# First set's row scores moved between the halves of the last projections

## The reference, cut to what matters

```python
x = L0_attn_a_query                                   # (2, 1024, 512) f32
x = x + _L0_attn_a_ref(_layernorm(x), Wq, Wk, Wv, Wout, lambdas, rms_weight)
x = x + _L0_ffn_ref(_layernorm(x), router_w, down_w, up_w)
x = x + _L0_attn_b_ref(_layernorm(x), ...)
x = x + _L0_ffn_ref(_layernorm(x), router_w, down_w, up_w)

# in _L0_attn_a_ref: H = 16 pairs of heads of D = 16
q = rotary((query @ Wq)); k = rotary((query @ Wk)); v = query @ Wv
attn1 = softmax(mask(q1 @ k1^T * D**-0.5)) @ v        # causal, first head of each pair
attn2 = softmax(mask(q2 @ k2^T * D**-0.5)) @ v        # second head of each pair
attn = lowpass_over_time(attn1 - lambda_full * attn2) # rfft, gaussian filter, irfft
attn = attn * rsqrt(mean(attn**2) + EPS) * rms_weight * (1 - LAMBDA_INIT)
return attn @ Wout
```

## Time and profile before

| | us |
|---|---|
| median of 3 runs | 1260.25 (1258.77 to 1263.32) |
| profiled execution | 1260.45 |
| its span, first to last instruction | 1258.7 |
| PE busy over the span | 1127.6 (90%) |
| DVE busy | 811.5 (64%) |
| POOL busy | 800.6 (64%) |
| ACT busy | 618.0 (49%) |
| mean granted clock of PE | 0.967 |

### The profile page before, as it was taken

How to read it: one execution, slowest core, us unless ns; L and a number is a source line. 1 busy time by engine, 2 the same in 40 slices (tenths; PEclk the granted TensorE clock), 3 DMA queues, 4 the chain that set the end, 5 groups by cost and what they waited for, 6 DMA issues and landing times. The chain is left out here.

```text
span 1258.7 us, 20791 instructions
## 1 busy us (share of the span) xinstructions
PE 1127.6 (90%) x7603; PEld 639.1 (51%) x7618; DVE 811.5 (64%) x1345; ACT 618.0 (49%) x1009; POOL 800.6 (64%) x584
## 2 busy tenths in 40 slices
PE   6999967989689889889898898897899999999996
PEld 5888722333234343343243243342367888887764
DVE  6887175565564665656557646643288788787786
ACT  4444215657557657656666564666642233332321
POOL 2012159569969879869879789668215677667321
PEclk9999959899889999999999998998999999999999
DMA  8333340120231220220221203103332322233651
GB/s 273 98 126 109 90 116 26 51 68 26 67 78 41 68 68 26 68 68 26 69 68 39 58 21 109 30 1 129 107 110 96 131 84 94 92 101 116 222 197 51
DMA packets 74836, 107.55 MB, mean 85 GB/s; under 512 B 12912, under 2 KB 36592, under 8 KB 74736
## 3 DMA queue, kind: packets, MB, share of 16 engines
q1 hardware_dynamic: 63616, 79.35, 21.4%
q0 software_dynamic: 4064, 14.16, 2.9%
q10 hardware_dynamic: 7056, 12.72, 2.7%
HBM read 68.44 MB, written 37.75 MB: 84 GB/s over the span
## 5 line engine op out<-in xcount | busy, mean ns | idle before, releaser
L1090 DVE TENSOR_REDUCE nm<-score 128x1 f32<-128x640 f32 (+6 forms) x352 | 349.4, 1025 | 272.6 <-PE score L981 220.8
L1257 POOL TENSOR_TENSOR base<-base,plain 128x2048 f32<-128x2048 f32 (+2 forms) x78 | 301.0, 3860 | 16.1 <-ACT plain L1206 6.2
L1206 ACT ACTIVATE plain<-score 128x1024 f32<-128x1024 f32 (+3 forms) x288 | 207.2, 734 | 108.4 <-PE score L997 60.4
L992 PE MATMUL score<-q,k 98*128 98x512 bf16 (+7 forms) x768 | 194.9, 340 | 51.7 <-ACT plain L1206 21.1
L992 PEld LDWEIGHTS score<-q,k 98*128 98x128 bf16 (+1 forms) x768 | 55.0, 99 | 155.1 <-DVE nm L1090 58.0
L1206 ACT ACTIVATE base<-score 128x1024 f32<-128x1024 f32 x96 | 97.5, 1023 | 72.9 <-PE score L997 51.6
L1010 PE MATMUL acc<-plain,vg 128*32 128x512 f32 (+3 forms) x1152 | 114.4, 470 | 0.0
L976 PE MATMUL score<-k,q 48*128 48x512 bf16 (+3 forms) x512 | 70.5, 355 | 17.7 <-DVE nm L1090 17.5
L1612 PE MATMUL m_b<-m_winh,m_hTh 128*128 128x512 f32 x192 | 83.6, 435 | 1.6 <-DVE m_k L1902 1.6
L1612 PE MATMUL m_b<-m_winh,m_hTl 128*128 128x512 f32 x192 | 75.8, 395 | 0.0
L1612 PE MATMUL m_b<-m_winl,m_hTh 128*128 128x512 f32 x192 | 75.7, 394 | 0.0
(11 more groups left out here) (312 smaller groups left out, 2514.3 us busy)
## 6 DMA issues: line engine op xcount, KB each, us to landing
q<-piece_scratch SPq DMA_DIRECT2D x192, 64.0 KB, 2.7
k<-piece_scratch SPq DMA_DIRECT2D x192, 64.0 KB, 2.3
piece_scratch<-n_pieces SPq DMA_DIRECT2D x16, 384.0 KB, 3.0
piece_scratch<-pieces POOLq DMA_DIRECT2D x8, 768.0 KB, 4.0
n_x1in<-in_query SPq DMA_DIRECT2D x16, 256.0 KB, 3.6
v_scratch<-n_v ACTq DMA_DIRECT2D x16, 256.0 KB, 2.2
vg<-v_scratch SPq DMA_DIRECT2D x8, 512.0 KB, 4.4
att_scratch<-m_qT SPq DMA_DIRECT2D x8, 512.0 KB, 3.0
```

The lines of the kernel that those rows point to most:

```text
L992: mm = nc.tensor.matmul(score[k % RING][:, x, t0:HALF], kst[n % SLOTS][c, first + x, j * P:(j + 1) * P], qst[n % SLOTS][c, first + x, h * ...
L1090: nc.vector.tensor_reduce(out, src, AX.X, ALU.max, negate=True).then_inc(s_max, 1)
L1206: nc.scalar.activation(tile_of(n, v)[:, first:first + 2, t0:HALF], score[k % RING][:, :, t0:HALF], ACT.Exp)\
L1257: nc.gpsimd.tensor_tensor(total, total, tile_of(n, v)[:, :, t0:HALF], ALU.add)\
```

## The change

Set 0's rows and maxima are made in the opening. `project` is split into two halves of six matmuls; rounds 18 to 20 put row steps behind the halves: steps 0 and 1 behind the second quarter (chunk 1) of round 18, then 2 and 3, then 4 and 5, and from round 19 one step behind each half, until step 13 at the end of round 20. That makes 11 places. Round 21's two projections follow alone. For PSUM the steps use the banks of transposes, of v, and of `pj[2:4]`, so that the last projections (from 26) alternate between two banks. DVE makes the maxima at the end of its rounds 18 to 20.

The stack of set 0 is filled by SP in round 15, after the store of projection 11, and the stack of set 1 at the end of the opening; its buffers `q1` and `k1` lie where the opening's `x` and `xn` were, so it waits for the last transpose. POOL writes its constant rows then. In attention, `schedule()` has no rows of set 0; all engines begin with the two shifts. POOL makes them right after clearing `shp`, and only the constant rows of slot 2 are left (four memsets). SP issues v of group 0 and 1 and the stack of set 2.

The diff, cut. The new `maxima`, `rows` and `slot_free` of the opening do what their namesakes in attention do.

```diff
-        self.q0, self.k0 = sb("q0", [P, GH, T], BF16), sb("k0", [P, GH, T], BF16)
+        self.q0, self.k0, self.q1, self.k1 = (sb(name, [P, GH, T], BF16) for name in ("q0", "k0", "q1", "k1"))
+        self.nm = sb("nm", [P, TB, GH])
...
+    FIRST_ROUND, FIRST_PAIRS, STACK_ROUND = 18, 3, 15
...
-        x = sb("x1in", [P, R, E])
-        xn = sb("xn", [P, R, E])
+        x, xn = early.q1[:].bitcast(F32), early.k1[:].bitcast(F32)
+        assert (R, E) == (GH, T // 2)
...
-        tp = [ctx.enter_context(nc.psum_tensor(f"n_tp{i}", [P, E], F32)) for i in range(RT)]
-        vp = [ctx.enter_context(nc.psum_tensor(f"n_vp{i}", [P, E], F32)) for i in range(RT)]
-        pj = [ctx.enter_context(nc.psum_tensor(f"n_pj{i}", [P, HALF], F32)) for i in range(RB)]
+        tps, vps, pjs = (ctx.enter_context(nc.psum_tensor("n_" + name, [P, n, HALF], F32))
+                         for name, n in (("tp", RT), ("vp", RT), ("pj", RB)))
+        tp, vp, pj = ([banks[:, i] for i in range(n)] for banks, n in ((tps, RT), (vps, RT), (pjs, RB)))
+        pairs = [tps[:], pjs[:, 2:4], vps[:]]
+        s_unit, s_max = sem("unit"), sem("max")
         s_win = [sem(f"win{i}") for i in range(3)]
         s_ident, s_wh, s_wl = sem("ident"), sem("wh"), sem("wl")
...
+        def bank_of(p):
+            return p % RB if p < 2 * (FIRST_ROUND + 1 - 6) else p % 2
+        def before(p):
+            return max([q + 1 for q in range(p) if bank_of(q) == bank_of(p)], default=0)
+        def first_steps(s, chunk):
+            c = 4 * (s - FIRST_ROUND) + chunk - 1
+            steps = range(2 * c, 2 * c + 2) if c < FIRST_PAIRS else [c + FIRST_PAIRS]
+            return [u for u in steps if 0 <= u < NRU]
...
+                if s == STACK_ROUND:
+                    for p in range(NTURN):
+                        if projection(p)[0] == 0:
+                            sp.wait_ge(s_first[p % RB], 16 * (p // RB + 1))
+                    early.stack(sp, piece_scr, early.q0, early.k0, 0)
             for i in range(RB):
                 sp.wait_ge(s_first[i], 16 * (NTURN // RB))
-            early.stack(sp, piece_scr, early.q0, early.k0, 0)
+            sp.wait_ge(s_tp, NT)
+            early.stack(sp, piece_scr, early.q1, early.k1, 1)
         @block.vector
...
+            def maxima(u):
...
             for s in range(NT + 6):
                 t = s
...
                     low_weight(WEIGHT_AT.index(s))
+                for chunk in range(4):
+                    for u in first_steps(s, chunk):
+                        maxima(u)
         @block.gpsimd
...
+            pool.wait_ge(s_tp, NT)
+            early.constant_rows(pool, nc.gpsimd, early.q1, early.k1, 4)
...
-            def project(p):
+            def slot_free(k):
+                if k >= RING:
+                    pe.wait_ge(s_max, k - RING + 1)
+                else:
+                    pe.wait_ge(*((s_xtl, NT), (s_raw, 2 * (FIRST_ROUND - 6)), (s_v, NT))[k])
+            def rows(u):
...
+            def project(p, half):
                 g, w, h, _ = projection(p)
                 q = p // (2 * G)
-                pe.wait_ge(s_xtl, QUARTER * (q + 1))
-                pe.wait_ge(s_wl, (w + 2) * KC)
-                if p >= RB:
-                    pe.wait_ge(s_raw, p - RB + 1)
+                if half == 0:
+                    pe.wait_ge(s_xtl, QUARTER * (q + 1))
+                    pe.wait_ge(s_wl, (w + 2) * KC)
+                    if before(p):
+                        pe.wait_ge(s_raw, before(p))
                 cols = slice(q % 2 * HALF, (q % 2 + 1) * HALF)
                 rows = slice(g % G * P, (g % G + 1) * P)
-                for c in range(KC):
+                for c in range(half * KC // 2, (half + 1) * KC // 2):
                     for n, (w_, x_) in enumerate(((wh, xth), (wh, xtl), (wl, xth))):
-                        mm = nc.tensor.matmul(pj[p % RB][:], w_[w + 1][:, c, rows], x_[:, c, cols],
+                        mm = nc.tensor.matmul(pj[bank_of(p)][:], w_[w + 1][:, c, rows], x_[:, c, cols],
                                               start=(c == 0 and n == 0), stop=(c == KC - 1 and n == 2))
-                mm.then_inc(s_pj, 1)
+                if half:
+                    mm.then_inc(s_pj, 1)
...
-                for p in of_round(s):
-                    project(p)
+                for chunk in range(4):
+                    for p in of_round(s)[chunk // 2:chunk // 2 + 1]:
+                        project(p, chunk % 2)
+                    for u in first_steps(s, chunk):
+                        if u == 0:
+                            pe.wait_ge(early.s_stack[0], 384)
+                            pe.wait_ge(early.s_const, 16 * 12)
+                        rows(u)
...
-                nc.scalar.copy(raw, pj[p % RB][:]).then_inc(s_raw, 1)
+                nc.scalar.copy(raw, pj[bank_of(p)][:]).then_inc(s_raw, 1)
...
-    line, start = [("rows", 0, u) for u in range(NRU)], []
+    line, start = [], []
     for n in range(SETS):
...
+    first = [("sums", 0, 0), ("sums", 0, 1)]
+    for h in range(2):
+        first += [("use", ("shift", 0, h), 0), ("evac", ("shift", 0, h), 0)]
     def put(k, event):
         behind.setdefault(k, []).append(event)
...
         g = n // 2
-        for h, last in enumerate((at["rows", n, FIRST_HALF - 1], at["rows", n, NRU - 1])):
+        for h, last in enumerate((at["rows", n, FIRST_HALF - 1], at["rows", n, NRU - 1]) if n else ()):
             put(last + PIECES_LATER, ("sums", n, h))
...
-    out = []
+    out = first
     for k, u in enumerate(line):
         out.append(u)
...
-            return n * ROW_SLOTS[NRU] + ROW_SLOTS[u + 1]
+            return (n - 1) * ROW_SLOTS[NRU] + ROW_SLOTS[u + 1]
...
-            stack(1)
             def weights_ahead():
...
                     take(("den", n, h))
+                if (n, h) == (0, 0):
+                    pe.wait_ge(s_ones, 11)
                 for v in terms:
                     if v in SUMS:
...
                         pe.wait_ge(s_vg[x // 2 % 2], 16 * (x // 4 + 1))
-                        pe.wait_ge(s_ones, 3 + 4 * SLOTS)
+                        pe.wait_ge(s_ones, 3 + 4 * SLOTS if x > 1 else 8)
...
                 c = slice(h * TB // 2, (h + 1) * TB // 2)
-                pool.wait_ge(s_max, rows_done(n, NRU - 1 if h else FIRST_HALF - 1))
                 if n >= 1:
+                    pool.wait_ge(s_max, rows_done(n, NRU - 1 if h else FIRST_HALF - 1))
                     pool.wait_ge(s_misc, order["shift", n - 1, h])
...
-                pool.wait_ge(s_ones, 5 + n)
-            for i in range(1, SLOTS):
+                pool.wait_ge(s_ones, 9 + n)
+                if n == 0:
+                    for h in range(2):
+                        shift_pieces(0, h)
+            for i in range(2, SLOTS):
                 early.constant_rows(pool, nc.gpsimd, qst[i], kst[i], 3 + 4 * i)
             for kind, x, u in EVENTS:
```

More of the change, by code:

```diff
@@ L418, in low_weight @@
                                              ALU.mult, ALU.subtract).then_inc(s_wl, 1)
+            def maxima(u):
+                i, heads = RU[u]
+                width = (i + 1) * P
+                for odd in range(fills("rows", u)):
+                    k = ROW_SLOTS[u] + odd
+                    bank = pairs[k % RING]
+                    dve.wait_ge(s_unit, k + 1)
+                    if width > HALF:
+                        src = bank.rearrange("p (o b) s -> p o (b s)", o=1)[:, :, 0:width]
+                        out = early.nm[:, i, heads[odd]:heads[odd] + 1].rearrange("p (a o) -> p a o", o=1)
+                    elif len(heads) == 2:
+                        src = bank[:, :, 0:width]
+                        out = early.nm[:, i, heads[0]:heads[1] + 1].rearrange("p (a o) -> p a o", o=1)
+                    else:
+                        src = bank[:, :, 0:2 * width].rearrange("p b (x s) -> p b x s", x=2)
+                        out = early.nm[:, i].rearrange("p (x b o) -> p b x o", b=2, o=1)
+                    vec.tensor_reduce(out, src, AX.X, ALU.max, negate=True).then_inc(s_max, 1)
             for s in range(NT + 6):
@@ L472, in _ @@
             pe.wait_ge(s_ident, 16)
-            def project(p):
+            def slot_free(k):
+                if k >= RING:
+                    pe.wait_ge(s_max, k - RING + 1)
+                else:
+                    pe.wait_ge(*((s_xtl, NT), (s_raw, 2 * (FIRST_ROUND - 6)), (s_v, NT))[k])
+            def rows(u):
+                i, heads = RU[u]
+                k, width, q0, k0 = ROW_SLOTS[u], (i + 1) * P, early.q0, early.k0
+                if width <= HALF:
+                    slot_free(k)
+                    each = len(heads) // 2
+                    banks = [pairs[k % RING][:, odd, 0:each * width].rearrange("p (a s) -> p a s", a=each)
+                             for odd in range(2)]
+                    for x in range(each):
+                        for odd in range(2):
+                            c, head = COARSE[odd], heads[2 * x + odd]
```

(31 more changed lines are left out.)

11 lines of the change are left out of this document (4 added, 7 removed).

## The result

The changed kernel takes 1249.36 us (median of 7 runs, 1246.27 to 1254.32) against 1261.42 for the kernel before (7 runs, 1258.77 to 1263.86). The ratio is 0.9923, 95% interval 0.9904 to 0.9942. The gain in the medians is 12.1 us; 11.75 was forecast. The profiled execution has a span of 1249.4 us.

A forecast was written before the change was run, and what follows sets the result against it. DVE's maxima bound set 0's rows, with PE half idle. Replacing 27.23 us by 9.1 + 1.28 + 5.6 = 15.98, plus 0.5, gains 11.75: from 1260.45 to 1248.7 us, range 1244 to 1255.5.

The forecast's parts named there:

- The removal and the sum: Last projection matmul to first probs: 27.23 us taken away, 15.98 put in its place, 11.25 gained, 11.75 with 0.5 more.
- part 2: PE in the opening: row steps 8.1 us plus shape changes 1.0, so it grows by 9.1 us (8.1 to 11.8).
- each change shows a whole tail: Rival on PE in the opening: 22 shape changes at 0.17 us, 3.7 instead of 1.0, giving 1251.4; chance 0.10.
- part 3: DVE in the opening: 21.5 us of maxima against 22.7 us of PE work, nearly even; cost 0, at most 1.5 us.
- part 4: SP's queue: stack 0 covered by over 12 us, stack 1 issued before the opening ends; cost 0.
- part 5: Block start to first probs: shift chain and v's landing both at 5.6 us (5.2 to 10.3).
- rival of v landing at 10.3: At attention's start, v of group 1 delays the first: gain cut by 4.7 us, 1253.4; longer new wait's chance 0.12.
- The barrier term: Last projection matmul's start to the block's start, taken as 1.28 us from the kernel before.
- The 0.5 us for the second half's shift: Inside set 0 in attention: PE work for that shift goes away, 0.5 us gained (0 to 1.1).
- part 6: POOL at attention's start: memsets end at 10.3 us after block start, first rotation at 12.4; covered by 2 us, cost 0.
- part 7: PE's clock at attention's start: falls after the barrier, returns some 5 us after the first probs; cost 0, 2.5 either way.
- the clock's 2.5 us: Rival at attention's start: clock does not fall after the barrier, 2.5 us less, 1246.2; clock luck below 1245.5 has chance 0.06.

The follow-up runs named there:

- change_again: The changed kernel unaltered, run once more beside others on the same chip, against the kernel before: 1246.62 us, ratio 0.9901.
- grain: The changed kernel with the row steps in 6 places behind whole projections instead of 11 behind halves: 1252.55 us, ratio 0.9947.
- one_round_later: The changed kernel with all row steps one round later, rounds 19 to 21, so no opening work stands behind the last step: 1250.63 us.
- shift_ready: The changed kernel with set 0's shift pieces cleared and cut by POOL in the opening, in an own buffer: 1247.47 us, ratio 0.9907.
- both_ready: The changed kernel with set 0's shift pieces cut and v of group 0 gathered in the opening: 1245.89 us, ratio 0.9891.
- shifts_inside: both_ready with set 0's shifts wholly made inside the opening's last two projections and ACT's table loaded before them: 1243.47 us, ratio 0.9883.
- both_warm: both_ready with ACT's table loaded at the opening's end and filler matmuls on PE before the first shifts: 1248.66 us, ratio 0.9925.

## Why the prediction was right

**The removal and the sum.** From the last projection matmul's old place to the first probs I had 9.1 + 1.28 + 5.6 = 15.98 us. Measured: 9.57 of growth, 162.71 - 161.06 = 1.65 to the block's start, 167.50 - 162.71 = 4.79 to the first probs, together 16.01. That the sum fits to 0.03 is partly luck: three terms are off by +0.5, +0.4 and -0.8. In `change_again` they are 9.58 (31.79 us from the last n_whv product of v to the last projection matmul, 22.21 before), 1.63 and 5.30, 0.5 more.

**PE in the opening** (part 2): 9.1 forecast, 9.57 measured, but the two terms were off in opposite ways. The way in takes 132.77 - 132.45 = 0.32 us where a matmul alone takes 0.227, and the way out 134.10 - 133.78 = 0.32 again: 0.1 us each. All 22 together take 2.1 us; I charged one of the two, 11 x 0.1 (1.1, put as 1.0), in the belief that the steps' prices held the other. The steps, from their first matmul to the next projection's first, take 7.25 us in the 11 places, where I had 8.1; most of the difference is in the narrow ones, 2.8 against 3.5. The last 0.2 us lie among the projections themselves. That the forecast came near is partly luck here, too. That each change shows a whole tail (3.7 us) is out: what a change between these two kinds of matmul costs here is 0.1 us.

**DVE** (part 3) was right: no wait of PE in the last rounds, last maximum at 158.30. `grain` and `one_round_later` show both covers at work, 4.6 and 1.7 us.

**SP's queue** (part 4): cost 0 and a wide cover, as put. The order of the loss when it goes was wrong: "one us for one us" is too little, since 2.24 us of stall cost 3.8 with the clock. And for stack 1 I argued only that its new place costs nothing, not that its old one would cost 9.2 us; that move is a condition of the gain, and a prediction without it would have had to be 5 to 8 us higher.

**From the barrier to the first probs** (part 5): the forecast that v and the shift chain end together was right; 5.6 was 0.8 high in one profile, 0.3 in the other. My rival of v landing at 10.3 is out: 5.87 in `shift_ready`. The barrier term, 1.28, was 1.65: I took it as fixed. The 0.5 us for the second half's shift does not show at set 0's first denominator (21.59 us behind the first probs, 21.42 before). At the second the change is 1.0 to 1.3 us nearer (51.01 and 51.39, 52.35 before), but the low clock before it also lasted longer in the kernel before (0.67 and 0.70 in 221 to 232), so no run shows this term. The forecast that the distance stays at 11 to 12 us to the end holds in neither profile.

**POOL** (part 6): its first rotation waits for DVE, not for its memsets, at 174.46, 7.0 us behind the first probs. The cover of 2 us was as small as put: with the first probs 1.9 us nearer to the block's start, in `both_ready`, POOL has no wait left between the block's start and this rotation (171.42).

**The clock** (part 7): 0.50 from the first probs to about 173, 5.6 us, 5.7 before: cost 0. It can be avoided, as `shifts_inside` shows, but no gain over `both_ready` is seen at set 0's first two denominators there. What I had no row for is the scatter in later sets: two profiles of one program differ by 4.7 us at the end of attention. All seven runs lie in the range, but a range from the priced terms alone, without the clock's 2.5 us, would have begun at 1246.7, above two of them (1246.27 and 1246.36). The chance of a time below 1254.0 adds up to 0.88 from its parts, not 0.87.

## What to carry to other kernels

Two stretches that each leave another engine idle can be laid over each other; the price is what the inserted work takes on the busier engine, and it can be read from rows at full clock before anything is built. Spread it as fine as the ring of buffers asks (half projections here), and leave as much busy-engine work behind the last piece as the slow engine needs for it. Then list every transfer that the old stretch hid: one of them is the next wait, and where two chains end together, only taking both away gains. A gain at the first instruction behind them can be gone 20 us later: look at a mark there before you count it.

## What the runs showed of the hardware

One stall of 2.24 us in an otherwise gapless stretch of TensorE was followed by its lower clock (0.62 mean over the next 4 us of full work), and so cost 3.8 us in all. Four waits of 0.95 to 1.35 us, 5 to 6 us apart, were not (1.00 over all of them, `grain`). A barrier of about 1.3 us with nothing else beside it did not lower the clock in `shifts_inside`; with the table load behind the last evacuation, 2.2 us of PE idle, it was low when PE began again in `both_warm`. After a rest of 3.4 us the same program began once at the full clock (first profile of the change) and once at the lower (`change_again`). What decides between such cases is left open.
